# A graph-attention and mixture-of-experts kernel: self-loop weights inside the two finishing stages, the first one written out per tile

## The reference, cut to what matters

```
e = jnp.exp(logits - m[dst])
denom = jax.ops.segment_sum(e, dst, num_segments=n)
alpha = e / denom[dst]
out = jax.ops.segment_sum(h[src] * alpha[:, :, None], dst, num_segments=n) + bias
...
h = gat_conv(x, W1, a_src1, a_dst1, b1, src, dst, HEADS, HID, concat=True)
h = jnp.where(h >= 0, h, prelu_w * h)
z = gat_conv(h, W2, a_src2, a_dst2, b2, src, dst, 1, OUT_CH, concat=False)
```

## Time and profile before

| | us |
|---|---|
| median of 3 executions | 5801.03 |
| lowest, highest | 5793.69, 5807.15 |
| the profiled execution | 5790.27 |
| its span | 5788.6 |
| busy: PE, PEld, DVE, ACT, POOL | 4371.0, 3233.2, 3235.0, 2815.7, 3552.6 |
| mean granted TensorE clock | 0.855 of full speed |

### The profile page before, as it was taken

One profiled execution on the slowest core, in us unless ns is written; L12 is line 12 of the kernel. 1 busy time (PEld: TensorE's weight loads), 2 busy tenths in 40 slices (PEclk: granted clock), 3 DMA queues, 4 the chain that ended last, 5 costly groups with the idle time before them and its releaser, 6 DMA issues. The chain is left out here.

```text
span 5788.6 us, 85756 instructions
## 1 busy us (share of the span) xinstructions
PE 4371.0 (76%) x20831; PEld 3233.2 (56%) x20831; DVE 3235.0 (56%) x8923; ACT 2815.7 (49%) x8615; POOL 3552.6 (61%) x3708
## 2 busy tenths in 40 slices
PE   7588888888888888656666666665665546999998
PEld 4466666666666666544444444444444434666666
DVE  5477777777677777754545454544444456222232
ACT  2576767677676766434444444433333342222222
POOL 0577777777777777017777777777777741233333
PEclk9798999999899899877788778777777766999999
DMA  5888888888888888235555555555666553411111
GB/s 184 244 242 247 240 240 242 240 245 241 240 246 238 242 239 246 85 118 141 144 143 142 139 144 143 140 136 156 164 166 170 158 149 105 142 49 51 51 51 39
DMA packets 689524, 975.33 MB, mean 168 GB/s; under 512 B 390410, under 2 KB 482408, under 8 KB 688798
## 3 DMA queue, kind: packets, MB, share of 16 engines
q0 software_dynamic: 228304, 716.77, 43.3%
q1 hardware_dynamic: 460190, 252.19, 15.8%
q10 hardware_dynamic: 560, 1.05, 0.1%
HBM read 899.62 MB, written 64.56 MB: 167 GB/s over the span
## 5 line engine op out<-in xcount | busy, mean ns | idle before, releaser
L859 POOL DMA_INDIRECT walk_ring<-s_h,walk_index x3320 | 3194.8, 962 | 1423.8 <-issue 928.3
L1020 PE MATMUL walk_pM<-walk_ring,walk_hit 128*128 128x262 f32 (+1 forms) x9960 | 2761.5, 430 | 13.0 <-ACT walk_ring L884 6.8
L1020 PEld LDWEIGHTS walk_pM<-walk_ring,walk_hit 128*128 128x128 f32 x9960 | 2026.4, 211 | 418.6 <-issue 73.2
L884 ACT ACTIVATE walk_ring<-walk_ring 128x128 f32<-128x128 f32 (+1 forms) x6640 | 2134.4, 414 | 5.4
L1250 DVE TENSOR_TENSOR acc<-walk_pM,acc 128x520 f32 (+1 forms) x1494 | 832.8, 557 | 584.0 <-PE walk_pM L1020 563.2
L874 ACT ACTIVATE walk_ring<-walk_gap 128x40 f32<-128x40 f32 (+1 forms) x249 | 54.1, 258 | 1898.6 <-DVE walk_gap L1212 1898.6
L924 PE MATMUL walk_pC<-all_ident,walk_best 128*84 128x128 f32 (+1 forms) x166 | 61.7, 372 | 1063.7 <-DVE walk_best L1168 986.0
L924 PEld LDWEIGHTS walk_pC<-all_ident,walk_best 128*84 128x84 f32 (+1 forms) x166 | 20.6, 124 | 1126.2 <-issue 1126.2
L1217 DVE TENSOR_TENSOR walk_hit<-walk_pK,walk_meta 128x512 f32<-128x512 f32 x830 | 560.7, 676 | 11.9
L2021 ACT ACTIVATE expert_hT<-expert_pG,expert_b 128x128 f32<-128x128 f32 x840 | 228.2, 382 | 615.7 <-PE expert_pG L2091 615.6
L1168 DVE TENSOR_TENSOR walk_best<-walk_ring,walk_dt 128x40 f32<-128x40 f32 (+1 forms) x249 | 47.2, 217 | 859.8 <-DMA walk_ring<-s_h,walk_index 859.8
(11 more groups left out here) (316 smaller groups left out, 4032.0 us busy)
## 6 DMA issues: line engine op xcount, KB each, us to landing
walk_hitT<-s_places SPq DMA_DIRECT2D x166, 640.0 KB
walk_ring<-s_h,walk_index POOLq DMA_INDIRECT x3320
expert_w<-in_fw_dram SPq DMA_DIRECT2D x16, 1024.0 KB, 6.5
walk_goal<-walk_target SPq DMA_DIRECT2D x830, 6.0 KB
walk_goal<-walk_target SPq DMA_DIRECT2D x830, 1.5 KB
walk_xk<-s_xT SPq DMA_DIRECT2D x98, 128.0 KB, 2.8
walk_resets<-s_resets SPq DMA_DIRECT2D x415, 20.0 KB
s_h<-first_h_out SPq DMA_DIRECT2D x7, 1056.0 KB, 4.3
```

What stands on the lines that cost most here:

```text
L859: pool.indirect_dma_start(ring[:, r % RS, t, :], None, table, bass.IndirectOffsetOnAxis(ap=index[:, r % TS, t:t + 1], axis=0)).then_inc(ro ...
L884: last = nc.scalar.activation(row, row, ACT.Copy, scale=ring[:, r % RS, t, at + FH:at + FH + 1])
L1020: last = nc.tensor.matmul(pM[:, b, a, 0:WIDE], hit[:, (r * CGROUPS + g) % HBUF, t % GROUP, :], ring[:, r % RS, t, a * HALF_ROW:a * HALF_RO ...
```

## The change

- `self_weights` becomes the class `SelfWeights`. Its tiles and semaphores belong to the finishing stage, and its two parts run at the beginning of DVE's and ACT's programs there. The two blocks of their own are gone, with their two resets of semaphores.
- `finish_layer1` is written out for all 49 tiles, without a loop or register waits. DVE's order is: slope, self-weights, `own` 0, `norm` 0, `own` 1, the attention columns, and then `norm` t, `own` t+1. `rows` and `h_out` get a second buffer of seven tiles; SP loads bias and slope, then rows(0), then the weights, then rows(1), and the rows of trip g+2 after the stores of trip g.
- The PReLU leaves DVE. ACT waits for its own two Relus and scales `neg` by -slope in place (L1503 of the new file); POOL adds `neg` and `pos` into `z` (L1439 of it), a `tensor_tensor` of 128x512.
- `finish_layer2` loads base(0) and rows(0) ahead of `wg`, `bg` and `valid`.
- `expert_pass` waits for `x_turned` >= 1 before it loads expert 1.

The diff, cut:

```
-                loads = [(w2..), (avec 0), (avec 1), (slope), (bias)]
...
+                for to, of in ((bias[:, :], d["b1"].partition_broadcast(P)), (slope[:, :], d["prelu_w"].partition_broadcast(P))):
+                    sp.dma_start(to, of).then_inc(bias_in, 16)
+                load_rows(0)
...
+                load_rows(1)
+                for g in range(TRIPS):
+                    for s, (lo, hi) in enumerate(UPARTS):
+                        sp.wait_ge(h_copied, g * U + hi)
...
+                    if g + 2 < TRIPS:
+                        load_rows(g + 2)
...
+            @block.gpsimd
+            def _(pool):
+                for t in range(NT):
+                    pool.wait_ge(neg_scaled, t + 1)
+                    if t >= 2:
+                        pool.wait_ge(multiplied, t - 1)
+                    nc.gpsimd.tensor_tensor(z[:, t % 2, :, :]..., neg[:, t % 2, :, :]..., pos[:, t % 2, :, :]..., ALU.add).then_inc(z_ready, 1)
...
+                def add_own(t):
+                    g, j = t // U, t % U
+                    if j in (0, UPARTS[0][1]):
+                        dve.wait_ge(rows_in[g % 2][part_of(j)], 16 * (g // 2 + 1))
+                    if t >= 2:
+                        dve.drain()
...
+                    last.then_inc(own_added, 1)
+
+                def normalise(t):
+                    if t >= 2:
+                        dve.wait_ge(turned, t - 1)
+                    dve.wait_ge(own_added, t + 1)
...
-                def prelu(i, t, j):
-                    after(dve, pos_ready, t + 1)
-                    after(dve, multiplied, i * U + max(j - 1, 0))
-                    nc.vector.scalar_tensor_tensor(out=z[:, j % 2, :, :], in0=neg[:, j % 2, :, :], scalar=slope[:, 0:1],
-                                                   in1=pos[:, j % 2, :, :], op0=ALU.mult, op1=ALU.add).then_inc(z_ready, 1)
...
+                share.on_vector(nc, dve, k, HEADS1, 2, F1, k["attn1"], acc)
+                add_own(0)
+                normalise(0)
+                add_own(1)
+                attention_weights()
+                for t in range(1, NT):
+                    normalise(t)
+                    if t + 1 < NT:
+                        add_own(t + 1)
...
+                    act.wait_ge(parts_ready, t + 1)
+                    nc.scalar.activation(neg[:, t % 2, :, :]..., neg[:, t % 2, :, :]..., ACT.Copy, scale=slope[:, 0:1]).then_inc(neg_scaled, 1)
...
+                share.on_scalar(nc, act)
+                act.wait_ge(share.share_ready, 1)
                 for t in range(2 * U):
                     weigh(t)
...
                     if e == 1:
-                        sp.wait_ge(x_turned, 2)
+                        sp.wait_ge(x_turned, 1)
```

More of the change, by code:

```diff
@@ L1312, in _ @@
                 loop(chunk)(dve)
[L1315 to L1367, removed]
@@ L1434, in _ @@
             @block.vector
             def _(dve):
-                nc.vector.memset(h_out[:, :, D + 1:], 0.0)
-                dve.wait_ge(weights_in, 16 * 5)
-                for s in range(2):
-                    nc.vector.tensor_tensor(aprod[:, :, :], w2[:, :, 0:D], spread(avec[:, s, :], 1, NB), ALU.mult)
-                    dve.drain()
-                    nc.vector.tensor_reduce(w2[:, :, D + s], aprod[:, :, :], AX_X, ALU.add)
-                    dve.drain()
-                nc.vector.tensor_scalar(slope[:, :], slope[:, :], -1.0, None, ALU.mult)
@@ L1451, in add_own @@
                         at = h // HP * HALF_ROW + h % HP * (P + 1)
-                        nc.vector.scalar_tensor_tensor(out=own[:, j % 2, h, :], in0=rows[:, j, at:at + P], scalar=k["self_share"][:, bass.ds(t, 1), h],
-                                                       in1=bias[:, h * P:(h + 1) * P], op0=ALU.mult, op1=ALU.add)
-                def normalise(i, t, j):
-                    b = j % 2
-                    after(dve, turned, i * U + max(j - 1, 0))
+                        last = nc.vector.scalar_tensor_tensor(out=own[:, t % 2, h, :], in0=rows[:, g % 2, j, at:at + P], scalar=k["self_share"][:, t, h:h + 1],
+                                                              in1=bias[:, h * P:(h + 1) * P], op0=ALU.mult, op1=ALU.add)
@@ new lines, in copy_out @@
+                def copy_out(t):
+                    g, j = t // U, t % U
+                    act.wait_ge(multiplied, t + 1)
+                    if g >= 2 and j in (0, UPARTS[0][1]):
+                        act.wait_ge(h_stored[g % 2][part_of(j)], 16 * (g // 2))
+                    nc.scalar.copy(k["attn2"][:, t, :], pH[:, t % 2, D:D + 2])
+                    nc.scalar.copy(h_out[:, g % 2, j, 0:D + 1], pH[:, t % 2, 0:D + 1]).then_inc(h_copied, 1)
+                for t in range(NT):
+                    parts(t)
+                    if t >= 1:
+                        copy_out(t - 1)
@@ L1509, in _ @@
+                copy_out(NT - 1)
             @block.tensor
             def _(pe):
[L1511 to L1526 removed]
@@ L1528, in _, with turn @@
-                with pe.Fori(0, TRIPS) as i:
-                    for j in range(U):
-                        turn(i, i * U + j, j)
-                        if j:
-                            multiply(i, i * U + j - 1, j - 1)
-                    multiply(i, i * U + U - 1, U - 1)
+                def turn(t):
+                    pe.wait_ge(normed, t + 1)
+                    if t >= 2:
+                        pe.wait_ge(parts_ready, t - 1)
+                    for b in range(NB):
+                        last = nc.tensor.transpose(pS[:, t % 2, b * P:(b + 1) * P], norm[:, t % 2, b, :], k["ident"][:, :])
+                    last.then_inc(turned, 1)
@@ new lines, in multiply @@
+                def multiply(t):
+                    pe.wait_ge(z_ready, t + 1)
+                    if t >= 2:
+                        pe.wait_ge(h_copied, t - 1)
+                    for b in range(NB):
+                        last = nc.tensor.matmul(pH[:, t % 2, 0:D + 2], z[:, t % 2, b, :], w2[:, b, :], start=(b == 0), stop=(b == NB - 1))
+                    last.then_inc(multiplied, 1)
+                turn(0)
+                pe.wait_ge(weights_ready, 1)
+                for t in range(NT):
+                    if t + 1 < NT:
+                        turn(t + 1)
+                    multiply(t)
@@ L1585, in finish_layer2 @@
         pI = m.ps("pI", [P, 512])
+        share = SelfWeights(m, 1)
         loads_in = m.sem("loads_in")
```

188 lines of the change are left out of this document (102 added, 86 removed).

## The result

The changed kernel takes 5779.8 us (median of 7 runs, 5772.9 to 5785.1) against 5798.0 for the kernel before on the same chip (7 runs, 5789.6 to 5807.2): 18.2 us less, ratio 0.997 with a 95% interval of 0.9958 to 0.9981. The forecast was 5787 and faster. The profiled execution took 5779.8, its span 5778.0.

The account below looks back on a forecast made before the run. Two untouched walks fill most of the span; within first-stage trips DVE's own order was the limit, plus 5.2 us per trip end. Terms -5.3 - 5.9 - 3 = -14.2 took the median of 5801.0 to 5787, range 5760 to 5804.

Parts of the forecast that it names:

- -5.3: First finishing stage: starts 9.0 us earlier but lasts 3.7 longer, 186.3 against 182.6, so 5.3 us less.
- Head of stage one, 9.0: First finishing stage's start: merged self-weights and reordered loads bring the first own 9.0 us earlier (7.5 to 10).
- Period 3.58: First finishing stage, each tile: DVE alone 2.57 us plus 1.01 lost to POOL's add, 3.58 against 3.73 before.
- loss per add: DVE beside POOL's add in the first finishing stage: 0.47 us seen per 256-wide add plus 0.54, so 1.01 per tile.
- DVE's wait for its own result: First finishing stage, each tile: 0.21 us, counted within DVE's own 2.57.
- The size of the add: POOL's 128x512 add: a quarter of 0.73 us taken as fixed, 0.54 per 256 elements, 1.27 in all (1.0 to 1.6).
- rival a: First finishing stage: adds fall into DVE's gaps, the two-tile loop rules, 2.94 us per tile, total 5757; 15%.
- Half clock, 2.0: First finishing stage's start: PE begins at half clock, one or two tiles at 4.9 us instead of 3.58, adding 2.0.
- Rival (c): First finishing stage: PE granted half clock, a tile costs 4.9 us, 63 more in all, total 5850; 7%.
- Rival (b): First finishing stage: add takes 1.6 us, or all of 1.27 is lost; period 3.84 to 3.9, total 5799 to 5802; 23%.
- Stage two, -5.9: Second finishing stage's head: base and rows load first, self-weights merged, so ACT starts 5.9 us earlier (4.5 to 7.5).
- Experts, -3: Experts' block: earlier loading of expert 1's weights removes a quarter of PE's stalls and slow clock, 3 us (0 to 8).

Follow-up runs that it names:

- e9: Changed kernel run again, unaltered, against the kernel before: 5774.6 against 5806.4 us, ratio 0.9951.
- e1: Changed kernel with the PReLU back on VectorE, POOL's add and ACT's scaling gone: 6712.7 against 6779.4 us for the kernel before, ratio 0.9896.
- e2: Changed kernel with POOL making each tile's add twice, a drain between: first own to last copy 224.0 us, one run 6783.6 us.
- e3: Changed kernel with POOL copying the negative part instead of adding, positive part left out: first own to last copy 143.8 us, one run 6701.0 us.
- e11: Changed kernel with own made by tensor_scalar from the rows alone, bias left out: first own to last copy 167.0 us, one run 5765.9 us.
- e4: Changed kernel with the self-weights in stages of their own again, at both places: ratio 0.9968 to the kernel before.
- e6: Changed kernel with the old order of loads in both finishing stages: first walk's end to next walk's start 204.9 us, against 200.4 in the changed kernel.
- e7: Changed kernel with expert 1's weights waiting for the second token tile again: experts' block 888.2 us, against 883.6 in the changed kernel.
- e8: Changed kernel with the attention columns made ahead of tile 0's own: first walk's end to next walk's start 203.1 us, against 200.4 in the changed kernel.

## Why the prediction was right, step by step

- **Faster, by the stages named: right.** I had -5.3, -5.9 and -3 (14.2); the profiles show -12.2, -5.9 and -4.9 (23.0). The 5787 was 7 us high against the first median, and the sum was 9 short of the stages.
- **Head of stage one, 9.0: under by 0.4 to 1.7.** The reset took 1.99, as worked out. Slope landed 3.3 after its issue, not 4.5, in the first profile. In e9 slope landed later, the `own` came at 14.0 and the gain is 9.4. Second `norm` after 8.18 (8.4).
- **Period 3.58: measured 3.485.** The loss per add was exactly the 1.01 of the sum, the add 1.26 to 1.27 undisturbed (1.27), and 1.37 to 1.42 in the steady rows. The term too large was DVE's wait for its own result: 0.10 behind a group of four, not the 0.21 of the earlier trace rows. 47 tiles of 0.095 are 4.5 us; with a few shorter spacings at the start the 47 came 5.2 under the sum. The size of the add was a guess, a quarter of it fixed, that hit. The two-tile loop (rival a) never set the pace: ahead of 47 of the 48 later `norm` DVE idles 0.10 to 0.12, its wait for its own result, and never for the PE.
- **Half clock, 2.0: too much.** The clock was at half for the first two turns and most of the first multiply (2.87 instead of 3.81), which DVE did not wait for; then 0.99. The last tile took 8.6 from its `norm` to its last copy (7.6), since that `norm` stood beside an add. Rival (c) had the direction wrong: the stage without trip ends had the higher clock. In the kernel before, the half clock lay behind the pauses at the trip ends and not in them: it was 0.50 from 2414.6 to 2424.7, where the second trip's tiles ran.
- **Rival (b), all of the add lost.** The Trainium skill (SBUF — State Buffer, Who interferes with whom) calls the ports that DVE and GpSimd share an exclusive lock, and says "fully blocks" of DVE's 2-port modes; by its word the period would have been 3.84. DVE lost 1.01 of 1.27, so the trace disagrees in the size. That POOL's operation holds DVE up is shown by e1, e2, e3 and e11.
- **Stage two, -5.9: right**, with first ACT row 11.0 and 10.7 after the walk (10.6). e4 and e6 split it: 3.7 for merging, 2.8 for the load order, each from one profile and with a scatter of B of up to 1.9.
- **Experts, -3: right in kind, low by 2.** e7 gives 4.6 for this edit alone. I had a quarter of the 8.3 us of stalls and of their slow clock; the stalls fell to 6.8 and 7.1. Where the rest of the 4.6 comes from is not shown.
- **What I did not see** is that the change holds a gain of some 38 and a loss of 25.5: A falls from 213.7 to 175.2 in e1, then rises to 200.4 with POOL. Of the 38, 6 came ahead of the second `norm`, which started 27.3 us after the walk before and 21.3 in e1. From there to the last `norm` the 47 spacings average 3.66 before and 2.96 in e1, 33 us in all, and that is the written-out loop with its doubled buffers (no trip ends, shorter drain). Taking back single parts of the head costs 7.6 (merging), 4.5 (load order) and 2.7 (attention columns), more than the 6, so these overlap. No kernel here had the loop alone undone.

## What to carry to other kernels

Where VectorE sets the pace, moving an operation from it to POOL pays only if POOL's price to VectorE is below what the operation costs there: here 1.01 us against 0.47, and the second is read from the starts of the neighbours, since an operation between two dependent groups fills their wait. Put work that needs no load over the first loads of a stage. Read a small edit from its own stretch of the trace when the rest of the program scatters more than the edit is worth.

## What the runs showed of the hardware

- VectorE is held up beside POOL's 128x512 add by 1.01 us of 1.27, whether its own operation is a `scalar_tensor_tensor` of two tensors (four take 2.15 instead of 1.14) or a `tensor_scalar` of one (1.90 instead of 0.87). A `TENSOR_REDUCE` beside the same add was not held up (1.22 each with and without it, the changed kernel and e8).
- A POOL copy of 128x512 (0.61 us) that lies wholly beside a group of VectorE costs it 0.35 to 0.43, and 0.18 to 0.30 where 0.40 to 0.51 of it do (e3). So the loss was not one share of POOL's operation: 1.01 of 1.27, 0.47 of 0.73 and 0.35 to 0.43 of 0.61 are each its undisturbed length less 0.18 to 0.26.
- A wait of VectorE for its own result behind a group of four cost 0.10 us, and 0.21 in the walk's accumulates.
- `norm` to `own` with a drain between takes 1.23 from start to start, with nothing to wait for 1.05.
- Two chips ran the walks 980 us slower; on one of them A of the same code was 200.5 us against 200.4 (e7 and the changed kernel), on the other B 190.8 against 190.9 (e2 and the changed kernel).
